# A DLRM tower with a third-order interaction network: another order in the first DMA queues, copies and picks, and picked lines with the row within the line innermost

## The chip, the cores and the metric

The kernel runs on one core of a Trainium2 chip. The metric is the device time of one execution in microseconds (us).

## What is computed

For each of 1024 samples, 32 embedding rows of 16 numbers are gathered from 32 tables. Three layers of a compressed interaction network follow, each a contraction of the outer product of the first rows with the last layer's rows, then a multi-layer perceptron:

```python
e = stack([tbl_m[ids[:, m]] for m in range(32)], axis=1)      # 1024 x 32 x 16
x0 = xk = e
for W in (W0, W1, W2):                                        # (32, 32 or 64, 64)
    xk = relu(einsum('bmd,bhd,mhk->bkd', x0, xk, W))
    outs.append(sum(xk, axis=2))
h = concatenate([*outs, dense_ctx], axis=1)                   # 1024 x 208
h = relu(h @ W_top1 + b_top1); h = relu(h @ W_top2 + b_top2); y = h @ W_top3
```

All of it is in float32. The tables have 1000, 1250, 12500 or 125000 rows.

## The kernel before

**Tiles and phases.** The batch is cut into eight tiles of 128 samples (i), each into two sides (A, Bs) of 64 samples, which are 1024 columns (sample, d). One side of one layer is a phase, written (i, layer, side). `PHASES` sets their order by hand: (0,0,A), (0,1,A), (0,0,Bs), (0,2,A), (0,1,Bs), (1,0,A), (0,2,Bs) and so on. In a phase the rows of xk lie in two PSUM banks, which ScalarE fills (`fill_first`, `fill_second`). VectorE multiplies them by slots of `x0rep`, the rows of x0 spread over the partitions (L1110), into a ring of six z buffers; GpSimd does some of the products of layers 1 and 2 (L554). TensorE multiplies each z by a tile of weights and accumulates (L753); in layer 0 the squares are added before the last step (L749). ScalarE copies the result out (`evacuate`, L861 and L867). VectorE waits to reuse a z buffer until TensorE has finished the step six before.

**Gathers and picks.** Each of the tables with 125000 or 12500 rows is read by indirect DMAs from GpSimd (L504). A small table can be picked instead: it is loaded whole as 125 lines of 8 or 10 rows (`load_lines`, L385). `split_ids` divides the indices into a line and a rest, `spread_lines` (L648) and `find_lines` (L1004) make a one-hot matrix of the lines, and `pick` (L662) multiplies it by the loaded lines. `clear_others` (L1031) multiplies the result by a mask of the row within the line, and `take_rows` (L1044) sums over the 8 or 10 rows. There are ten such groups, q = 0 to 9: six of tile 0, which need all six groups of lines, and four of tile 1. `pick_rows(q)` on VectorE is clear_others(q), find_rows(q+1), find_lines(q+2), take_rows(q).

**The round trip of tile 0.** SyncE saves the even rows of tile 0 to `x0_rows` in HBM once the gathers of those rows have landed and picks 0 to 2 are taken (`save_first(0)`, L457), waits until they have landed, and loads the even slots of side A (`load_x0`, L428). Then it loads six pieces of w0, and does the same for the odd rows, which need picks 0 to 5. The two first bank fills of phase (0,0,A) do not wait for this trip: TensorE turns the rows (`turn_rows`, L677), ScalarE copies them (`copy_rows`, L784) and TensorE selects them (`select_rows`, L689). Phase (0,0,A) uses slots 0, 2, 1 and 1, so its third product needs the first odd slot. After the odd slots come rows, lay and the eight slots of side Bs (`load_side`), the weights of the perceptron (L470 to L475), and tile 1's save (L405).

**Weights.** w0 is summed from w0a and w0b on VectorE, written twice to HBM (`w0_twice`, L400), and loaded in 16 pieces with rotations (`load_w0`, L379), ten by ScalarE's queue and six by SyncE's. w1 and w2 are each loaded in 12 pieces, eight straight from the input (`STRAIGHT`) and four from a copy in HBM with shifted tiles, `w1_wrap` and `w2_wrap` (`make_wrap`, L765; `load_w`, L776). ScalarE's queue issues them all: w1's between the two copy_rows and after the second; w2's behind the bank fills of phase (0,1,A), where ScalarE then waits for the copy to land. Behind w2's loads stands ctx (L937), and behind that ScalarE's work for phase (0,0,Bs). TensorE waits for w1_in before phase (0,1,A), for w2_in before (0,2,A).

**Order on TensorE at the start.**

```python
spread_lines(6)
pick(3)
turn_rows(0)
pick(4)
spread_lines(7)
select_rows(0)
pick(5)
```

## Time and profile before

| | us |
|---|---|
| median of 3 runs | 629.13 |
| lowest and highest | 628.42, 631.07 |
| the profiled execution | 629.63 |
| its span | 627.7 |
| TensorE, VectorE busy | 585.6 (93%), 577.4 (92%) |
| GpSimd, ScalarE busy | 497.3 (79%), 349.6 (56%) |
| mean granted clock of TensorE | 0.984 |

The span is what the profile covers; 1.9 us of the execution's time lie around it. Of the 95.36 MB that the DMA engines move, 90.55 MB are in the queue of SyncE and 2.41 MB in that of ScalarE. A timeline row shows a run of like instructions with the start of the first; the idle time in brackets is that of the engine before it, with what ended it, and "issue" there means that the profile shows nothing that the engine waited for, often its own DMA issues.

### The profile page before, as it was taken

Reading aid. Unit: us, or ns where it says so; the run is one execution under the profiler, and the core shown is the slowest. Engines: PE = TensorE matmul, PEld = TensorE weight load, DVE = VectorE, ACT = ScalarE, POOL = GpSimd, SP = SyncE. Lnnn points to the kernel's source line nnn. Section 1 sums busy time; section 2 is a strip of 40 time slices with the busy share of each in tenths; the row PEclk is TensorE's granted clock in tenths of the full one; section 3 lists DMA queues with packets and bytes.
Section 4 is the critical chain, followed back from the end, with each engine's and each line's share of the span. In section 5 each row is a group of like instructions: output and inputs, shape, how many; then the busy total and the mean of one; then the engine's idle time right before and its main releaser. Section 6 shows DMA issues by size and latency. Waiting matters only on the chain. (4 is left out here: it accounts for less than half of the span.)

```text
span 627.7 us, 8728 instructions
## 1 busy us (share of the span) xinstructions
PE 585.6 (93%) x3126; PEld 214.1 (34%) x3126; DVE 577.4 (92%) x582; ACT 349.6 (56%) x535; POOL 497.3 (79%) x349
## 2 busy tenths in 40 slices
PE   3485689999999899999999999999999999999998
PEld 3361223222442224322342224322442234333444
DVE  5567599899999999999999999999999999999993
ACT  0105174745755667635755666635755666756741
POOL 6753579799888988899888988898888896668770
PEclk9879979999999999999999999999999999999999
DMA  4689979940499928993599727980699728990000
GB/s 110 129 165 236 251 119 272 294 118 4 77 237 224 191 19 185 231 240 58 81 243 247 159 28 198 296 210 3 114 236 242 138 28 202 237 247 3 1 2 1
DMA packets 89326, 95.36 MB, mean 152 GB/s; under 512 B 59597, under 2 KB 68338, under 8 KB 89282
## 3 DMA queue, kind: packets, MB, share of 16 engines
q1 hardware_dynamic: 78590, 90.55, 62.8%
q0 software_dynamic: 7104, 1.83, 3.9%
q10 hardware_dynamic: 3588, 2.41, 1.5%
q8 instruction: 25, 0.41, 0.3%
q14 instruction: 19, 0.16, 0.1%
HBM read 91.35 MB, written 3.94 MB: 152 GB/s over the span
## 5 line engine op out<-in xcount | busy, mean ns | idle before, releaser
L1110 DVE TENSOR_TENSOR z<-xk,x0rep 128x1024 f32<-128x1024 f32 x457 | 522.9, 1223 | 19.8 <-issue 9.6
L753 PE MATMUL acc<-z,w_sb 128*64 128x512 f32 x1828 | 433.6, 599 | 20.4 <-DVE z L1110 17.3
L554 POOL TENSOR_TENSOR z_pool<-x0rep,xk_copy 128x1024 f32<-128x1024 f32 x119 | 283.3, 2381 | 55.7 <-PE acc L753 27.9
L504 POOL DMA_INDIRECT emb<-tbl,idx x222 | 213.0, 959 | 58.4 <-issue 48.3
L753 PEld LDWEIGHTS acc<-z,w_sb 128*64 128x64 f32 x1828 | 123.7, 137 | 294.9 <-issue 161.2
L847 ACT ACTIVATE xk<-xk_copy 32x1024 f32<-32x1024 f32 x128 | 130.5, 1019 | 94.3 <-DVE z L1110 93.1
L753 PE MATMUL acc<-z_pool,w_sb 128*64 128x512 f32 x476 | 122.5, 593 | 0.0
L861 ACT ACTIVATE xk_copy<-acc 64x512 f32<-64x512 f32 x128 | 75.2, 588 | 3.7 <-PE acc L753 2.2
L842 ACT ACTIVATE xk<-lay 128x1024 f32<-128x1024 f32 x15 | 15.4, 1027 | 75.7 <-DVE z L1110 75.7
L753 PEld LDWEIGHTS acc<-z_pool,w_sb 128*64 128x64 f32 x476 | 33.7, 137 | 65.1 <-issue 62.8
L823 ACT ACTIVATE xk<-xk_copy 128x1024 f32<-128x1024 f32 x31 | 31.9, 1028 | 14.2 <-DVE z L1110 13.9
L1083 DVE TENSOR_REDUCE row_sums<-layer_out 128x32 f32<-128x512 f32 x47 | 32.2, 684 | 0.0
L805 ACT ACTIVATE squares<-squares 32x1024 f32<-32x1024 f32 x16 | 16.8, 1050 | 23.4 <-issue 14.5
L867 ACT ACTIVATE layer_out<-acc 128x512 f32<-128x512 f32 x47 | 27.8, 591 | 2.1 <-PE acc L753 1.4
L879 ACT ACTIVATE in<-row_sums 64x32 f32<-64x32 f32 x94 | 21.3, 227 | 4.7 <-DVE row_sums L1083 3.6
L1031 DVE TENSOR_TENSOR x0rep<-acc,mask 128x480 f32<-128x480 f32 (+1 forms) x10 | 6.7, 666 | 14.2 <-PE acc L662 14.2
L662 PE MATMUL acc<-x0rep 125*128 125x160 f32 (+1 forms) x68 | 14.8, 377 | 4.9 <-DMA x0rep<-tbl 4.9
L749 PE MATMUL acc<-squares,w0d_sb 128*64 128x512 f32 x64 | 16.9, 606 | 0.4
L823 ACT ACTIVATE xk<-lay 128x1024 f32<-128x1024 f32 x15 | 15.4, 1028 | 2.8 <-DMA lay<-x_rows 2.4
L784 ACT ACT_TABLE_LOAD x1 | 1.3, 1283 | 27.5 <-issue 27.5
L662 PEld LDWEIGHTS acc<-x0rep 125*128 125x128 f32 x68 | 12.6, 259 | 7.9 <-DMA x0rep<-tbl 5.3
L590 PEld LDWEIGHTS top<-h,wt_sb 128*64 128x64 f32 x224 | 12.7, 137 | 4.0 <-issue 4.0
(67 smaller groups left out, 140.6 us busy)
## 6 DMA issues: line engine op xcount, KB each, us to landing
x0rep<-x_rows SPq DMA_DIRECT2D x128, 512.0 KB, 20.7
lay<-x_rows SPq DMA_DIRECT2D x30, 512.0 KB, 6.9
emb<-tbl,idx POOLq DMA_INDIRECT x222, 3.5
squares<-x_rows SPq DMA_DIRECT2D x16, 128.0 KB, 8.6
x_rows<-emb SPq DMA_DIRECT2D x7, 256.0 KB, 4.6
x_rows<-emb SPq DMA_DIRECT2D x9, 128.0 KB, 5.9
w_wrap<-w ACTq DMA_DIRECT2D x4, 128.0 KB, 9.7
w_sb<-w ACTq DMA_DIRECT2D x8, 64.0 KB
```

Source lines behind the costliest of these rows:

```text
L504: pool.indirect_dma_start(out=emb[:, i % 2, m, :], out_offset=None, in_=tables[m], in_offset=bass.IndirectOffsetOnAxis(ap=idx[:, i, m:m + ...
L554: pool.tensor_mul(z_pool[:, (count - 1) % POOL_RING, :], x0rep[:, g % X0_GROUPS, slot, :], xk_copy[:, side, :]).then_inc(z_pool_ready, 1)
L662: op = pe.matmul(acc[:, ACC_AT[q], t * n * D:(t + 1) * n * D], hots[:, q % HOTS, t * P:(t + 1) * P], lines[:, ALL_PICKED.index(m), 0:n * D ...
L749: pe.matmul(bank[c * H:(c + 1) * H, :], w0d_sb[:], squares[:, side, c * COLS:(c + 1) * COLS], start=False, stop=False)
L753: mm = pe.matmul(bank[c * H:(c + 1) * H, :], w[:, tile, :], src[:, c * COLS:(c + 1) * COLS], start=(k == 0), stop=last)
L823: act.activation(xk[:, 0, :], src, ACT.Copy).then_inc(xk_ready[0], 1)
L847: op = act.activation(xk[q * Q:(q + 1) * Q, 1, :], xk_copy[other * Q:(other + 1) * Q, side, :], ACT.Copy)
L861: op = act.activation(xk_copy[half * H:(half + 1) * H, side, c * COLS:(c + 1) * COLS], bank[c * H:(c + 1) * H, :], ACT.Relu)
L867: act.activation(layer_out[:, n % OUTS, :], bank, ACT.Relu).then_inc(acc_taken, 1)
L879: op = act.activation(dst[:, at:at + ROWS], row_sums[c * H:(c + 1) * H, i % 2, row, :], ACT.Copy)
L1083: dve.tensor_reduce(row_sums[:, i % 2, SUM_ROWS.index((layer, side)), :], layer_out[:, n % OUTS, :].rearrange("p (b d) -> p b d", d=D), AX ...
L1110: dve.tensor_mul(z[:, (count - 1) % RING, :], xk[:, bank, :], src).then_inc(z_ready, 1)
```

## The change

It has four parts. In the pick, the loaded lines are read with the row within the line innermost, so that the product in PSUM, its masked copy and the sum in `take_rows` have the rows to be summed next to each other. On SyncE the lines of group 0 come before w0a and w0b, only tile 1's indices come early (a semaphore of their own, `idx_second_in`), the two writes of w0_twice come after the lines of group 1, and behind the last lines come w1_wrap's copies and the rest of the indices. SyncE issues w0's pieces 12 to 15, of which two stand before its wait for the even rows, and makes w2_wrap ahead of side Bs. On ScalarE w0's pieces 8 to 11 and half of w1's straight pieces come before the second copy_rows, the other half after it, and w1's wrapped pieces after the first square. TensorE does picks 3, 4 and 5 earlier, and VectorE splits tile 1's indices after pick 2.

```diff
@@ -200,7 +200,7 @@
 FIRST_GATHERS = [[m for m in GATHERED[0] if m % 2 == odd] for odd in range(2)]
 FIRST_SAVES = 4
 
-W0_LOADS = 10
+W0_LOADS = 12
 
 LOADED_BY_ACT = (0, 2, 18, 22, 4, 8, 7, 13, 23, 25)
 N_TOP_LOADS = 6
@@ -378,6 +379,12 @@
                 tiles = w0_sb[r::PER_GROUP, 0:TILES0:TILES0 - 1, :] if shift % 2 == 0 else w0_sb[r::PER_GROUP, 1:3, :]
                 queue.dma_start(tiles, rows.rearrange("(g e) k -> g e k", e=2)).then_inc(w0_in, 16)
 
+        def make_wrap(queue, wrap, src, done):
+
+            for at, t in ((0, TILES - WRAP // 2), (WRAP // 2, 0)):
+                queue.dma_start(bass.AP(wrap, at * H, [[WRAP * H, P], [1, WRAP // 2 * H]]),
+                                src[:, t:t + WRAP // 2, :].rearrange("p t k -> p (t k)")).then_inc(done, 16)
+
         def load_lines(queue, by_act, g):
 
             for m in of_group(g)[0]:
@@ -389,15 +396,18 @@
         def _(sp):
 
             sp.dma_start(idx[:, 0, :], ids[0:P, :]).then_inc(idx_first_in, 16)
+            load_lines(sp, False, 0)
             for dst, src in ((w0a_sb, w0a), (w0b_sb, w0b)):
                 sp.dma_start(dst, src).then_inc(w0ab_in, 16)
-            load_lines(sp, False, 0)
-            sp.dma_start(idx[:, 1:NT, :], ids[P:B, :].rearrange("(t p) m -> p t m", p=P)).then_inc(idx_in, 16)
-            for g in range(1, len(PICKED)):
-                load_lines(sp, False, g)
+            sp.dma_start(idx[:, 1, :], ids[P:2 * P, :]).then_inc(idx_second_in, 16)
+            load_lines(sp, False, 1)
             sp.wait_ge(w0_summed, 2)
             for n in range(2):
                 sp.dma_start(w0_twice[:, n, :].rearrange("q (r t k) -> q r t k", r=M, t=TILES0), w0a_sb).then_inc(w0_twice_in, 16)
+            for g in range(2, len(PICKED)):
+                load_lines(sp, False, g)
+            make_wrap(sp, w1_wrap, w1, w1_wrap_in)
+            sp.dma_start(idx[:, 2:NT, :], ids[2 * P:B, :].rearrange("(t p) m -> p t m", p=P)).then_inc(idx_in, 16)
 
             def save_x0(i, lo, hi, row, done):
 
@@ -455,17 +465,21 @@
                 for lo, hi, row in ((0, M, odd), (0, X_ROWS - M, M + odd)):
                     dst = bass.AP(x0_rows, row * PITCH, [[D, P], [2 * PITCH, (hi - lo) // 2], [1, D]])
                     sp.dma_start(dst, emb[:, 0, lo + odd:hi:2, :]).then_inc(saved_first, 16)
-                sp.wait_ge(saved_first, 32 * (odd + 1))
 
             save_first(0)
+            sp.wait_ge(w0_twice_in, 32)
+            load_w0(sp, W0_LOADS, W0_LOADS + 2)
+            sp.wait_ge(saved_first, 32)
             for slot in range(0, SLOTS, 2):
                 load_x0(0, A, slot)
-            load_w0(sp, W0_LOADS, TILES0 * P // M)
+            load_w0(sp, W0_LOADS + 2, TILES0 * P // M)
             save_first(1)
+            sp.wait_ge(saved_first, 64)
             for slot in range(1, SLOTS, 2):
                 load_x0(0, A, slot)
                 if slot == 1:
                     load_rows(0, A)
+            make_wrap(sp, w2_wrap, w2, w2_wrap_in)
             load_side(0, Bs)
             sp.dma_start(wt1_sb[:, 0, :], wt1[0:P, :]).then_inc(top_in, 16)
             sp.dma_start(wt1_sb[0:K3, 1, :], wt1[P:P + K3, :]).then_inc(top_in, 16)
@@ -519,7 +533,7 @@
             for g, group in enumerate(FIRST_GATHERS):
                 for m in group:
                     gather(0, m, gathered_first[g])
-            pool.wait_ge(idx_in, 16)
+            pool.wait_ge(idx_second_in, 16)
             for m in GATHERED[1]:
                 gather(1, m, gathered[1])
 
@@ -528,6 +542,7 @@
                 if m == 0:
 
                     if j == 2:
+                        pool.wait_ge(idx_in, 16)
                         pool.wait_ge(saved_first, 16 * FIRST_SAVES)
                     else:
                         pool.wait_ge(x0_saved[j % 2], 32 * ((j - 1) // 2))
@@ -660,7 +675,8 @@
                     pe.wait_ge(cleared_out, earlier_user(ACC_AT, q))
                 for t, m in enumerate(group):
                     op = pe.matmul(acc[:, ACC_AT[q], t * n * D:(t + 1) * n * D], hots[:, q % HOTS, t * P:(t + 1) * P],
-                                   lines[:, ALL_PICKED.index(m), 0:n * D], start=True, stop=True)
+                                   lines[:, ALL_PICKED.index(m), 0:n * D].rearrange("p (j d) -> p d j", d=D),
+                                   start=True, stop=True)
                 op.then_inc(picked, 1)
 
             def turn_rows(odd):
@@ -698,15 +714,15 @@
             pick(1)
             spread_lines(5)
             pick(2)
+            pick(3)
+            pick(4)
             spread_lines(6)
-            pick(3)
             turn_rows(0)
-            pick(4)
+            pick(5)
             spread_lines(7)
             select_rows(0)
-            pick(5)
+            pick(6)
             spread_lines(8)
-            pick(6)
             turn_rows(1)
             pick(7)
             spread_lines(9)
@@ -759,12 +775,6 @@
 
         @block.scalar
         def _(act):
-            def make_wrap(wrap, src, done):
-
-                for at, t in ((0, TILES - WRAP // 2), (WRAP // 2, 0)):
-                    act.dma_start(bass.AP(wrap, at * H, [[WRAP * H, P], [1, WRAP // 2 * H]]),
-                                  src[:, t:t + WRAP // 2, :].rearrange("p t k -> p (t k)")).then_inc(done, 16)
-
             def load_w(dst, src, tiles, done, pieces):
 
                 half = SLOTS // 2
@@ -789,14 +799,12 @@
             act.wait_ge(cleared, 1)
             act.dma_start(w0d_sb[0:M, :], w0d).then_inc(w0d_in, 16)
             act.wait_ge(w0_twice_in, 32)
-            load_w0(act, 0, W0_LOADS - 2)
+            load_w0(act, 0, 8)
             copy_rows(0)
-            load_w0(act, W0_LOADS - 2, W0_LOADS)
-            make_wrap(w1_wrap, w1, w1_wrap_in)
-            load_w(w1_sb, w1.tensor, TILES, w1_in, STRAIGHT)
+            load_w0(act, 8, W0_LOADS)
+            load_w(w1_sb, w1.tensor, TILES, w1_in, STRAIGHT[:2])
             copy_rows(1)
-            act.wait_ge(w1_wrap_in, 32)
-            load_w(w1_sb, w1_wrap, WRAP, w1_in, WRAPPED)
+            load_w(w1_sb, w1.tensor, TILES, w1_in, STRAIGHT[2:])
 
             def square(i, side):
 
@@ -805,6 +813,8 @@
                 act.activation(of_side, of_side, ACT.Square).then_inc(squares_ready, 1)
 
             square(0, A)
+            act.wait_ge(w1_wrap_in, 32)
+            load_w(w1_sb, w1_wrap, WRAP, w1_in, WRAPPED)
 
             def fill_first(n):
                 if PHASES[n] in TURNED:
@@ -928,7 +938,6 @@
                     take_h2(before_top)
                 fill_second(n)
                 if n == 1:
-                    make_wrap(w2_wrap, w2, w2_wrap_in)
 
                     act.wait_ge(x0_in[0][SLOTS - 1], 16)
                     load_w(w2_sb, w2.tensor, TILES, w2_in, STRAIGHT)
@@ -1028,17 +1037,18 @@
                 dve.wait_ge(picked, q + 1)
                 dve.wait_ge(masked, q + 1)
                 wide = count * n * D
-                dve.tensor_tensor(chosen[:, q % 2, 0:wide].rearrange("p (r d) -> p r d", d=D),
-                                  acc[:, ACC_AT[q], 0:wide].rearrange("p (r d) -> p r d", d=D),
-                                  mask[:, q % 2, 0:count * n].unsqueeze(2).to_broadcast([P, count * n, D]), ALU.mult
-                                  ).then_inc(cleared_out, 1)
+                shape = [P, count, D, n]
+                dve.tensor_tensor(chosen[:, q % 2, 0:wide].rearrange("p (t d j) -> p t d j", d=D, j=n),
+                                  acc[:, ACC_AT[q], 0:wide].rearrange("p (t d j) -> p t d j", d=D, j=n),
+                                  mask[:, q % 2, 0:count * n].rearrange("p (t j) -> p t j", j=n).unsqueeze(2).to_broadcast(shape),
+                                  ALU.mult).then_inc(cleared_out, 1)
 
             def take_rows(q):
 
                 i, g = PICKS[q]
                 _, count, n, _ = of_group(g)
                 dve.wait_ge(cleared_out, q + 1)
-                rows = chosen[:, q % 2, 0:count * n * D].rearrange("p (t j d) -> p t d j", j=n, d=D)
+                rows = chosen[:, q % 2, 0:count * n * D].rearrange("p (t d j) -> p t d j", j=n, d=D)
                 at = 0
                 for run in PICKED[g]:
                     op = dve.tensor_reduce(run_of(emb[:, i], run), rows[:, at:at + len(run)], AX_X, ALU.add)
@@ -1066,9 +1076,10 @@
             last = P - M
             dve.tensor_add(w0a_sb[0:last, TILES0 - 1, :], w0a_sb[0:last, TILES0 - 1, :],
                            w0b_sb[0:last, TILES0 - 1, :]).then_inc(w0_summed, 1)
-            dve.wait_ge(idx_in, 16)
-            split_ids(1)
             for q in range(7):
+                if q == 3:
+                    dve.wait_ge(idx_second_in, 16)
+                    split_ids(1)
                 pick_rows(q)
 
             dve.wait_ge(w0_twice_in, 32)
```

How the order moves on TensorE around pick 5 (L662 and L677 are the picks, L648 and L663 the spread, L689 and L705 select_rows). Before:

```order
L662 MATMUL acc<-x0rep 128x160 x3
L677 MATMUL xk<-ident_f,emb 16x64 x16
L662 MATMUL acc<-x0rep 128x160 x3
L648 MATMUL top<-ident_b,line 125x128 x4
L689 MATMUL xk<-lay,select 64x512 x4
L662 MATMUL acc<-x0rep 128x160 x3
L648 MATMUL top<-ident_b,line 125x128 x3
```

And in the changed kernel:

```order
L677 MATMUL acc<-x0rep 128x160 x9
L663 MATMUL top<-ident_b,line 125x128 x4
L693 MATMUL xk<-ident_f,emb 16x64 x16
L677 MATMUL acc<-x0rep 128x160 x3
L663 MATMUL top<-ident_b,line 125x128 x4
L705 MATMUL xk<-lay,select 64x512 x4
L677 MATMUL acc<-x0rep 128x128 x4
```

Pick 5 stood behind the first select_rows and now stands right behind turn_rows.

SyncE's queue from the last tables (x0rep<-tbl, 125x160) to the save of the odd rows (the second pair of x_rows<-emb). Before:

```order
L385 DMA x0rep<-tbl 125x160 x6
L400 DMA w_twice<-z 4x32x256 x2
L457 DMA x_rows<-emb 128x16x16
L457 DMA x_rows<-emb 128x8x16
L428 DMA x0rep<-x_rows 128x1x1024 x4
L379 DMA w_sb<-w_twice 16x2x64 x6
L457 DMA x_rows<-emb 128x16x16
L457 DMA x_rows<-emb 128x8x16
```

And in the changed kernel:

```order
L406 DMA w_twice<-z 4x32x256 x2
L392 DMA x0rep<-tbl 125x160 x6
L385 DMA w_wrap<-w 128x256 x2
L410 DMA idx<-ids 128x6x32
L467 DMA x_rows<-emb 128x16x16
L467 DMA x_rows<-emb 128x8x16
L380 DMA w_sb<-w_twice 16x2x64 x2
L438 DMA x0rep<-x_rows 128x1x1024 x4
L380 DMA w_sb<-w_twice 16x2x64 x2
L467 DMA x_rows<-emb 128x16x16
L467 DMA x_rows<-emb 128x8x16
```

The two copies into w_wrap and most of the indices are now ahead of the even save, and four instead of six w0 pieces ahead of the odd one.

ScalarE from the last of w1's loads, behind the second copy_rows, to the load of ctx; w1 stands before the fill L831 or L841 and w2 behind it. Before:

```order
L776 DMA w_sb<-w_wrap 32x1x256 x4
L805 ACTIVATE squares<-squares 32x1024
L831 ACTIVATE xk<-acc 64x512 x2
L861 ACTIVATE xk_copy<-acc 64x512 x4
L867 ACTIVATE layer_out<-acc 128x512
L847 ACTIVATE xk<-xk_copy 32x1024 x4
L765 DMA w_wrap<-w 128x256 x2
L776 DMA w_sb<-w 64x1x256 x2
L776 DMA w_sb<-w 32x1x256 x4
L776 DMA w_sb<-w 64x1x256 x2
L776 DMA w_sb<-w_wrap 32x1x256 x4
L937 DMA in<-ctx_t 16x128
```

And in the changed kernel:

```order
L786 DMA w_sb<-w 64x1x256 x2
L813 ACTIVATE squares<-squares 32x1024
L786 DMA w_sb<-w_wrap 32x1x256 x4
L841 ACTIVATE xk<-acc 64x512 x2
L871 ACTIVATE xk_copy<-acc 64x512 x4
L877 ACTIVATE layer_out<-acc 128x512
L857 ACTIVATE xk<-xk_copy 32x1024 x4
L786 DMA w_sb<-w 64x1x256 x2
L786 DMA w_sb<-w 32x1x256 x4
L786 DMA w_sb<-w 64x1x256 x2
L786 DMA w_sb<-w_wrap 32x1x256 x4
L946 DMA in<-ctx_t 16x128
```

The copies into w_wrap are gone from this queue, and w1's loads from w_wrap stand behind the square.

## Rows read from the trace of the kernel before

**Rows 1.** Windows: stretch, length, busy us of PE, PEld, DVE, ACT, POOL, clock, DMA share, GB/s.

```profile
26.00:38.00 12.00, 6.51 (x20) 3.29 (x21) 2.41 (x6) 2.29 (x2) 9.02 (x10) 0.53 1.00 222
...
62.00:78.00 16.00, 10.52 (x48) 3.35 (x48) 9.26 (x9) 2.02 (x3) 9.36 (x7) 1.00 1.05 252
...
78.00:90.00 12.00, 9.78 (x34) 3.05 (x36) 11.65 (x11) 11.79 (x18) 7.90 (x6) 0.72 0.89 143
...
110.00:627.00 517.00, 508.62 (x2736) 177.70 (x2732) 497.66 (x464) 315.52 (x494) 426.08 (x284) 1.00 0.66 145
```

**Rows 2.** Timeline, VectorE: start, us, line, operation, count [idle before <- releaser].

```profile
10.59 0.40 DVE L985 TENSOR_SCALAR quotient<-idx 128x32 f32<-128x32 int32 x2 [3.40 <-DMA idx<-ids]
...
35.42 0.66 DVE L1031 TENSOR_TENSOR x0rep<-acc,mask 128x480 f32<-128x480 f32 x1 [9.87 <-PE acc L662]
...
48.37 2.36 DVE L1110 TENSOR_TENSOR z<-xk,x0rep 128x1024 f32<-128x1024 f32 x2 [0.36 <-DMA x0rep<-x_rows]
...
78.15 4.62 DVE L1110 TENSOR_TENSOR z<-xk,x0rep 128x1024 f32<-128x1024 f32 x4 [6.88 <-issue]
...
82.97 9.14 DVE L1110 TENSOR_TENSOR z<-xk,x0rep 128x1024 f32<-128x1024 f32 x8 [0.20 <-ACT xk L823]
...
119.15 3.49 DVE L1110 TENSOR_TENSOR z<-xk,x0rep 128x1024 f32<-128x1024 f32 x3 [2.63 <-ACT xk L823]
```

**Rows 3.** Timeline, SyncE's queue: start, us that the issues took, line, count.

```profile
24.42 3.66 SPq L428 DMA_DIRECT2D x0rep<-x_rows  x4
...
37.91 2.63 SPq L457 DMA_DIRECT2D x_rows<-emb  x2
...
42.94 0.55 SPq L428 DMA_DIRECT2D x0rep<-x_rows  x1
```

**Rows 4.** DMA issues at 24.6 to 25.8 and at 37 to 39: KB each, us to landing.

```profile
x0rep<-x_rows SPq DMA_DIRECT2D x3, 512.0 KB, 9.8
...
x_rows<-emb SPq DMA_DIRECT2D x1, 128.0 KB, 4.3
```

**Rows 5.** Timeline, TensorE's matmuls.

```profile
51.69 1.03 PE L753 MATMUL acc<-z,w_sb 128*64 128x512 f32 x4
...
55.59 4.38 PE L753 MATMUL acc<-z,w_sb 128*64 128x512 f32 x16 [2.88 <-DVE z L1110]
...
62.81 1.08 PE L753 MATMUL acc<-z,w_sb 128*64 128x512 f32 x4 [2.84 <-DVE z L1110]
...
79.52 5.39 PE L753 MATMUL acc<-z,w_sb 128*64 128x512 f32 x12 [6.19 <-DVE z L1110]
...
87.36 2.79 PE L753 MATMUL acc<-z,w_sb 128*64 128x512 f32 x12 [0.70 <-DMA w_sb<-w_wrap]
```

**Rows 6.** Timeline, ScalarE and its queue.

```profile
41.88 2.60 ACTq L776 DMA_DIRECT2D w_sb<-w_wrap  x4
...
49.55 1.05 ACT L805 ACTIVATE squares<-squares 32x1024 f32<-32x1024 f32 x1 [6.66 <-DMA squares<-x_rows]
...
56.88 0.56 ACTq L765 DMA_DIRECT2D w_wrap<-w  x1
...
70.68 5.23 ACTq L937 DMA_DIRECT2D in<-ctx_t  x1
...
75.95 1.05 ACT L805 ACTIVATE squares<-squares 32x1024 f32<-32x1024 f32 x1 [14.52 <-issue]
```

**Rows 7.** The tile w_wrap: time from issue to landing of its four copies.

```profile
DMA to landing us min/median/max: 8.9/9.7/10.6
```

**Rows 8.** Groups: busy us, mean ns | idle before; the last by shape, 0 to 52 us.

```profile
L842 ACT ACTIVATE xk<-lay 128x1024 f32<-128x1024 f32 x15 | 15.4, 1027 | 75.7 <-DVE z L1110 75.7
...
L1083 DVE TENSOR_REDUCE row_sums<-layer_out 128x32 f32<-128x512 f32 x47 | 32.2, 684 | 0.0
...
L662 PE MATMUL acc<-x0rep 125*128 125x160 f32 (+1 forms) x68 | 14.8, 377 | 4.9 <-DMA x0rep<-tbl 4.9
...
L1044 DVE TENSOR_REDUCE emb<-x0rep 128x64 f32<-128x512 f32 x2 | 2.0, 1000 | 0.0
```

More of the change, by code:

```diff
@@ L298, in build @@
         idx_first_in = sem("idx_first_in")
+        idx_second_in = sem("idx_second_in")
         idx_in = sem("idx_in")
```

## The prediction, made before the changed kernel ran

> **What bounds the kernel now.** I read the windows first. From 110 us to the end TensorE is busy for 508.62 of 517.00 us and VectorE for 497.66, at a full clock and with the DMA engines at 0.66 [rows 1]. Nothing in the diff touches an instruction of that stretch, so the change can only move the moment at which it begins; what it brings is the shift of the whole steady part. Before it things look different: from 26 to 38 us VectorE works 2.41 of 12 us while the DMA engines are at 1.00 and TensorE's clock at 0.53, and from 62 to 78 us the DMA share is 1.05 with TensorE busy 10.52 of 16 [rows 1]. So the second view is VectorE's timeline, for the waits that end late. It waits 3.40 us for the indices, 9.87 us for a pick at 35.42, then for the first odd slot of x0rep (the product at 48.37), 6.88 us before 78.15, and 2.63 us before 119.15 [rows 2]. A wait counts only if nothing else would have held the next step. For that I read SyncE's queue: even slots issued from 24.42, save of the odd rows at 37.91, first odd slot at 42.94 [rows 3]. That last chain leads straight to 48.37. The 6.88 us have another origin: ScalarE fills the banks for phase (0,0,Bs) only after its queue has issued everything for w2, and there it waits 14.52 us of issue, until 75.91 [rows 6].
>
> **The change part by part.** The sum is made against the profiled execution, 629.63 us; the median of the runs shown is 629.13, 0.5 below.
>
> *Indices and lines.* idx for tile 1 comes alone and split_ids(1) moves behind pick 2. The 3.40 us go from VectorE, but the even save is still held by the queue: the order of SyncE now has two w1_wrap copies and the rest of the indices ahead of it, some three more issues of about 0.65 us, as four of 2.60 us show [rows 6], and their bytes. In the old order the lines and w0_twice stood there. I take 24.42 for the even landing unchanged: term 0, bounds -3 (the wait gone in full) and +2 (three issues and the copies' bytes in front).
>
> *Sums over neighbours.* A take of 512 elements costs 1000 ns with the lines' rows outermost [rows 8]; a reduction of as many contiguous elements costs 684 ns [rows 8]. Over ten picks, at up to 1.0 us each, this frees about 3 us of VectorE, all of it before the product at 48.37, which waits for a DMA. What hides it is the x0_rows round trip; term 0, and if that cover went, -3. The other side of the same edit: the 68 pick matmuls, busy 14.8 us together [rows 8], now read their moving operand with a stride of 64 bytes. The trace has no such matmul. Bounds: nothing, or twice the time, which for the 40 of the first six picks is 40 x 14.8/68 = 8.7 us more. I take nothing, since between picks TensorE waits anyway (9.87 us on VectorE's side come from elsewhere); the high end would put picked_out 6 near 33, still ahead of the odd save's turn below. The Trainium skill (SBUF — State Buffer, "Door 1: The DMA port swizzle") says that consecutive SBUF accesses run at full rate only inside a 16-byte line, so that fp32 is free up to a stride of four. The pair 1000 and 684 ns agrees with it, and by that rule the matmuls pay, and the sum stays as it is because they are covered.
>
> *Pick 5 ahead of select_rows(0).* Pick 5 was stuck behind select_rows(0), which waited for ScalarE's copy. It now runs right behind turn_rows(0), and VectorE ends pick 5 near 24 to 26 instead of after its product of 35.42 [rows 2]. SyncE gets to the odd save after four slot loads (3.66 us from 24.42) and two of the former six w0 loads, at about 29 instead of 37.91 [rows 3]: 8 to 9 us earlier. That is one bound. The other is the DMA: the even slots issued at about 25 land 9.8 us later [rows 4], in a stretch at share 1.00 [rows 1], and the odd save stands behind them in the same queue. With w1's straight loads now beside them I expect the slots done at 36 to 37, and with 4.3 us for the save [rows 4] the odd rows land near 41 instead of 42.94. Bounds -8.5 and 0; I take -2, because the share of 1.00 is the nearer row.
>
> *TensorE's clock.* With the picks over by about 37, TensorE idles until the first odd slot. At 78.15 the trace shows what a gap does: 6.19 us idle, and then 12 matmuls in 5.39 us, where 12 at 87.36 take 2.79 [rows 5]; the granted clock is 0.72 from 78 to 90 [rows 1]. The tail of phase 0 is 12 such matmuls, which end at 52.72 [rows 5]. If the clock is at its lower level there, +2.6 at most, and if not, 0. I take +2. So phase 0 ends about where it does now.
>
> *w1_wrap's loads behind square(0, A).* Four issues, 2.60 us [rows 6], move behind a square that waits for the odd rows. Behind them on ScalarE stands the first fill of phase 1. The square ran from 49.55 to 50.60 [rows 6] and the fill can start at 52.72, so the delay is about half a microsecond: term 0. When they land is the first rival.
>
> *w2_wrap's copies on SyncE.* ScalarE no longer issues them at 56.88 nor waits for them; that wait ended near 68, since four more loads, 2.60 us, came before ctx at 70.68 [rows 6]. Its twelve loads at 0.65 us each are now done near 65. Then comes the load of ctx, which took 5.23 us to issue [rows 6], because the queue was full; I keep that, so ScalarE is free near 71 instead of 75.91: 5 us. The product at 82.97 came 7.06 us behind 75.91; it would come near 78.2. The limit of this term is TensorE, whose last matmul of phase 1 ends at 79.52 - 6.19 = 73.33 [rows 5]. Three activations of about 1.03 us [rows 8] no longer stand between it and the copy-out, so 73.33 + 7.06 - 3.1 = 77.3 is the earliest: bounds -5.7 and 0, taken -4.7.
>
> *w2_in.* TensorE waits for it until 87.36 [rows 5]. The last of twelve loads was issued just before ctx at 70.68 [rows 6], 16.7 us earlier. The two copies that stood ahead of them landed 9.7 us after their issue [rows 7]; without them the twelve gain between 0 and 9.7 us, and I take the middle, 4.5, since their bytes still pass the same engines from SyncE's queue. From there to 119.15 TensorE has no gap, so its -4.5 and VectorE's -4.7 are one gain, not two.
>
> *Last wait of the indices, POOL, tile 1.* GpSimd's gathers of tile 2 also wait for idx_in, issued before 20 us and used after 40: 0. Tile 1's rows come from the same queue, and between 82.97 and 119.15 VectorE's only longer wait is one for ScalarE [rows 2]: 0.
>
> Sum: 0 + 0 - 2 + 2 + 0 - 4.5 = -4.5, that is 625.1 against the profiled run and **624.6** against the median.
>
> **The rivals.** *A, w1 late (slower).* Place: TensorE's wait for w1_in before phase 1. Its first four products took from 55.59 to 59.97, and then it idled 2.84 us until 62.81 [rows 5]; so it bears a start up to 59.3. The wrapped loads were issued at 41.88; now at about 50 to 53. With 9.7 us to landing [rows 7] w1_in comes at 62, with the 16.7 us of w2's at 69. In the latter case phase 1 ends 10 us later, w2's gain is covered by it, the idle gap adds some 2.6 us of low clock, and the product of 82.97 comes near 90: 629.1 + 7 = 636. At 62 about 2.7 us (62 less 59.3) and a low clock are lost and the total is 627 to 629. For it: the queue of SyncE is full when they go out, as at 62 to 78 with a share of 1.05 [rows 1]. Against it: the loads are small, and at 41.88 they had landed before 55.59.
> *B, the round trip is freed.* SyncE's order decides and not the bytes: -8.5 at the odd save, no cold clock, then -4.5: 616.
> *C, ScalarE's queue gets its share.* The Trainium skill (DMA: Bandwidth & Descriptors, "Queues, rings and completion order") says that each engine takes turns between queues packet by packet. As a mechanism here: the twelve loads no longer wait behind SyncE's, so w2_in comes 9 us earlier, and then 77.3 and the 2.63 us before 119.15 [rows 2] are what is left to gain: 5.7 + 2.6 = 8.3, 621. Rows 7 speak against it with 9.7 us for two copies of 128 KB.
> *D, nothing.* ctx's issue ends when the DMA backlog ends, at 75.9 whatever stands before it, and the change moves no bytes away: 629.
>
> **How the numbers follow.** A difference of 0.5%, 3.1 us, is about what a measurement of this kernel can tell from none. Forecast 0.40, A 0.14 (its worse half slower, its better half the same), B 0.13, C 0.13, D 0.20. Faster by over 0.5%, below 626.0: B, C and most of the forecast, with an edge of D, 0.60. Slower, above 632.3: 0.12. The rest, 0.28, is within 0.5%. The range goes from B's edge, 617, to 631: A's worse half and the outer part of B are left out. The forecast alone stands at 621.5 to 627.5.
>
> **What would show it.** VectorE's 9.87 us before pick 5 gone; takes of 512 elements near 0.68 us; the odd save issued near 29 but landed near 41; a product at about 46.5 with a long DMA wait before it; a lower clock around 50; ScalarE free at about 71; the products of (0,2,A) from about 78; w2_in near 83. It is wrong if the odd save lands before 38 (B), if TensorE's first matmul of phase 1 comes after 60 (A), if w2_in comes before 80 (C), or if ctx's issue still ends at 75 to 76 (D).

## The result and the profile after

The changed kernel takes 633.14 us in the median of 9 runs (629.83 to 635.59), the kernel before 629.66 us of 9 (628.42 to 632.04). The ratio is 1.0045, with a 95% interval of 1.0024 to 1.0066: about 0.45% slower, inside the 0.5% called "same" in the prediction, and above the end of its range (631.0). The forecast of 624.6 was wrong in sign.

The profiled execution of the changed kernel is the lowest of its nine runs, 629.83 us with a span of 628.0; that of before took 629.63. The spans alone would say that nothing happened. So the start is compared by its milestones; why the spans agree is told in the last part.

VectorE's timeline of the changed kernel (start, us, line, operation, count, in brackets the idle time before it and what ended it), which answers to [rows 2]:

```profile
14.22 0.67 DVE L1054 TENSOR_REDUCE emb<-x0rep 128x64 f32<-128x512 f32 x1
...
25.98 0.66 DVE L1041 TENSOR_TENSOR x0rep<-acc,mask 128x480 f32<-128x480 f32 x1 [0.67 <-PE acc L677]
...
47.02 2.36 DVE L1121 TENSOR_TENSOR z<-xk,x0rep 128x1024 f32<-128x1024 f32 x2 [6.80 <-DMA x0rep<-x_rows]
...
53.21 1.42 DVE L1105 TENSOR_SCALAR xk<-acc 64x512 f32<-64x512 f32 x2 [2.58 <-PE acc L769]
...
76.00 4.62 DVE L1121 TENSOR_TENSOR z<-xk,x0rep 128x1024 f32<-128x1024 f32 x4 [0.15 <-issue]
...
85.67 9.14 DVE L1121 TENSOR_TENSOR z<-xk,x0rep 128x1024 f32<-128x1024 f32 x8 [5.06 <-ACT xk L833]
...
121.15 1.23 DVE L1121 TENSOR_TENSOR z<-xk,x0rep 128x1024 f32<-128x1024 f32 x1 [1.93 <-ACT xk L833]
```

The take of 512 elements is down to 0.67 us; the 9.87 us before pick 5 are down to 0.67 (the row of 25.98), and a wait of 6.80 us for the first odd slot stands in their place. The product at 47.02 is 1.35 us earlier than before. The product for (0,0,Bs) is earlier too, at 76.00 instead of 78.15. But the one for (0,2,A), behind a wait for ScalarE's fill, starts at 85.67 instead of 82.97, and the one near 120 at 121.15 instead of 119.15. These last 2.0 us are what the start lost.

SyncE's queue of the same kernel, against [rows 3]:

```profile
25.17 3.29 SPq L438 DMA_DIRECT2D x0rep<-x_rows  x4
...
29.88 7.95 SPq L467 DMA_DIRECT2D x_rows<-emb  x2
41.56 0.55 SPq L438 DMA_DIRECT2D x0rep<-x_rows  x1
```

The save of the odd rows is issued from 29.88 instead of 37.91, and the first odd slot follows at 41.56 instead of 42.94: the queue gave 8 us and the DMA engines kept 6.6 of them.

TensorE's matmuls, against [rows 5]:

```profile
48.30 1.97 PE L769 MATMUL acc<-z,w_sb 128*64 128x512 f32 x4 [5.10 <-DVE z L1121]
50.06 1.92 PE L765 MATMUL acc<-squares,w0d_sb 128*64 128x512 f32 x4
...
65.78 6.37 PE L769 MATMUL acc<-z,w_sb 128*64 128x512 f32 x20 [12.62 <-DMA w_sb<-w_wrap]
...
88.62 2.79 PE L769 MATMUL acc<-z,w_sb 128*64 128x512 f32 x12 [2.73 <-DMA w_sb<-w_wrap]
```

Phase 1 began at 55.59; now it waits 12.62 us for w1's wrapped pieces, until 65.78. The second wait is for w2, and it ends at 88.62 instead of 87.36. ScalarE and its queue, against [rows 6]:

```profile
47.86 2.60 ACTq L786 DMA_DIRECT2D w_sb<-w_wrap  x4
...
62.84 8.19 ACTq L786 DMA_DIRECT2D w_sb<-w_wrap  x4
71.07 2.68 ACTq L946 DMA_DIRECT2D in<-ctx_t  x1
73.80 1.05 ACT L813 ACTIVATE squares<-squares 32x1024 f32<-32x1024 f32 x1 [11.91 <-issue]
```

and of before, the row that [rows 6] does not have:

```profile
68.05 2.60 ACTq L776 DMA_DIRECT2D w_sb<-w_wrap  x4
```

w1's four loads of 32 KB leave at 47.86 to 50.5 and are there at 65.78, over 15 us later. w2's four wrapped loads now begin at 62.84 instead of 68.05, but their issue takes 8.19 us instead of 2.60, so that the last is out at 71.03, where before it was out at 70.65. ScalarE stands free 2.15 us earlier (73.80 instead of 75.95), for ctx takes 2.68 instead of 5.23 us. The windows (stretch, length, busy us of PE, PEld, DVE, ACT, POOL, clock, DMA share, GB/s), against [rows 1]:

```profile
26.00:38.00 12.00, 12.00 (x78) 8.52 (x76) 8.15 (x18) 1.01 (x1) 9.20 (x10) 0.86 1.05 211
...
50.00:62.00 12.00, 3.16 (x10) 0.70 (x6) 6.68 (x8) 8.17 (x11) 4.55 (x3) 0.64 1.05 239
```

From 26 to 38 us VectorE works 8.15 us instead of 2.41, and from 50 to 62 us TensorE is busy for 3.16 us of 12, at a granted clock of 0.64, with a DMA share of 1.05.

### The profile page after: what moved, and what is told of

Same layout as the page of the kernel before. It is cut to its first block, busy times and chain, and to the rows that moved or that the text cites. A ratio compares the mean times of both kernels' runs of the same rounds, so it can differ in the third digit from the quotient of the medians.

```text
span 628.0 us, 8730 instructions
## 1 busy us (share of the span) xinstructions
PE 589.0 (94%) x3126; PEld 218.8 (35%) x3126; DVE 574.4 (91%) x582; ACT 349.9 (56%) x535; POOL 497.1 (79%) x349
## 4 chain that ended last, share of the span: by engine, by line
PE 44%; DVE 10%; issue 2%; ACT 1%; DVEq 0%
PE acc L769 39%; DVE z L1121 9%; PE top L605 1%; PE acc L765 1%; DVE row_sums L1094 1%; PE top L596 1%; PE top L593 1%; ACT xk L833 1%; PE acc L645 0%; ACT xk L852 0%; PE top L614 0%; PE xk L633 0%; PE xk L625 0%; PE top L580 0%; PE top L650 0%
## 5 line engine op out<-in xcount | busy, mean ns | idle before, releaser
L1121 DVE TENSOR_TENSOR z<-xk,x0rep 128x1024 f32<-128x1024 f32 x457 | 524.5, 1260 | 25.8 <-ACT xk L833 7.0
L769 PE MATMUL acc<-z,w_sb 128*64 128x512 f32 x1828 | 433.9, 600 | 25.8 <-DMA w_sb<-w_wrap 15.4
L769 PEld LDWEIGHTS acc<-z,w_sb 128*64 128x64 f32 x1828 | 125.1, 137 | 299.9 <-issue 168.5
L1094 DVE TENSOR_REDUCE row_sums<-layer_out 128x32 f32<-128x512 f32 x47 | 33.9, 721 | 0.0
L677 PE MATMUL acc<-x0rep 125*128 125x160 f32 (+1 forms) x68 | 18.8, 436 | 5.8 <-DMA x0rep<-tbl 5.8
L677 PEld LDWEIGHTS acc<-x0rep 125*128 125x128 f32 x68 | 15.1, 263 | 9.0 <-DMA x0rep<-tbl 6.3
L605 PE MATMUL top<-h,wt_sb 128*64 128x128 f32 x224 | 13.4, 273 | 0.0
```

What stands on the lines that cost most here:

```text
L605: last = pe.matmul(top[halves[half], m * P:(m + 1) * P], wt2_sb[:, k, columns_of(m, half)], h1[:, k, :], start=(k == 0), stop=(k == F1 // ...
L677: op = pe.matmul(acc[:, ACC_AT[q], t * n * D:(t + 1) * n * D], hots[:, q % HOTS, t * P:(t + 1) * P], lines[:, ALL_PICKED.index(m), 0:n * D ...
L769: mm = pe.matmul(bank[c * H:(c + 1) * H, :], w[:, tile, :], src[:, c * COLS:(c + 1) * COLS], start=(k == 0), stop=last)
L1094: dve.tensor_reduce(row_sums[:, i % 2, SUM_ROWS.index((layer, side)), :], layer_out[:, n % OUTS, :].rearrange("p (b d) -> p b d", d=D), AX ...
L1121: dve.tensor_mul(z[:, (count - 1) % RING, :], xk[:, bank, :], src).then_inc(z_ready, 1)
```

## The experiments

Open were the cost of w1's late loads, why w2 did not come earlier, and which of the two sets the end. "w1 ahead" puts w1's wrapped loads back ahead of the square; "w2 on SyncE" takes w2's loads out of ScalarE's queue. Each ratio is against the kernel before on the same chip. The chips are numbered in the order of these runs; the first comparison is not counted among them.

### First chip: parts alone

w1 ahead, in the changed kernel:

```diff
             load_w(w1_sb, w1.tensor, TILES, w1_in, STRAIGHT[2:])
+            act.wait_ge(w1_wrap_in, 32)
+            load_w(w1_sb, w1_wrap, WRAP, w1_in, WRAPPED)
...
             square(0, A)
-            act.wait_ge(w1_wrap_in, 32)
-            load_w(w1_sb, w1_wrap, WRAP, w1_in, WRAPPED)
```

> The changed kernel with one thing put back: w1's four wrapped loads stand ahead of the first square again. Theory 'w1 late' (the 12.62 us for which TensorE waits before phase (0,1,A) are what the change gives back): that wait is gone, phase 1's first matmul comes at about 54.7 as the z of the changed kernel allow (54.67), its last near 74. Then w2_in is the next bound: its loads were last seen to land at 88.6, so phase (0,2,A) starts on TensorE at 84 to 88, and the kernel is 2 to 6 us faster than the changed one, 627 to 631. Rival 'another cause' (the wait is covered, or the picks' new layout or the queue order costs it): it stays within 1 us of the changed kernel, 632 to 634.

Measured: 650.33 us against 653.54, 0.9951 (0.9924 to 0.9977). Here the edit did not take the wait away: its loads go out only from 62.14, and TensorE still waits 13.40 us for them, until 85.28. So this run says nothing of what that wait costs.

With w2's two copies on ScalarE's queue again (`make_wrap(sp, w2_wrap, ...)` back to `make_wrap(act, ...)` behind the fills):

> e1_w1_ahead, and w2_wrap's two copies back on ScalarE's queue, as in the kernel before. Theory 'the copies on SyncE free ScalarE' (my term of -4.7 us): ScalarE's square for (0,0,Bs) goes back from about 72 to 75 or later, the products of (0,0,Bs) start 3 to 5 us later than in e1_w1_ahead. If w2_in decides the end of it, the total is only 0 to 2 us above e1_w1_ahead; if ScalarE decides, 4 us above. Rival 'w2's data are what counts': with the copies back on ScalarE's queue w2_in lands later by the bytes' time, 1 to 5 us, and so does the total.

Measured: 1.0018 (0.9993 to 1.0043), 0.7% above the one without it. On this chip the copies on SyncE did help.

The kernel before, with w1's wrapped loads behind the square (the first diff the other way round):

> The kernel before with only w1's four wrapped loads moved behind the first square. Theory 'w1 late': issued at about 50.6 they land at 60 to 68; TensorE bears a start of phase 1 up to 59.3, so phase 1 ends 1 to 9 us later; with the low clock the kernel is 3 to 9 us slower than before, 632 to 638. Rival 'it needs the rest of the change' (w2's copies on SyncE ahead of side Bs push them back): they land before 60 and the time stays at 629 to 630.

Measured: 1.0056 (1.003 to 1.0083).

The changed kernel with the old layout of the pick in the matmul, the masking and the take:

```diff
-                                   lines[:, ALL_PICKED.index(m), 0:n * D].rearrange("p (j d) -> p d j", d=D),
+                                   lines[:, ALL_PICKED.index(m), 0:n * D],
...
-                rows = chosen[:, q % 2, 0:count * n * D].rearrange("p (t d j) -> p t d j", j=n, d=D)
+                rows = chosen[:, q % 2, 0:count * n * D].rearrange("p (t j d) -> p t d j", j=n, d=D)
```

> The changed kernel with the old layout of the picks (row within the line outermost, sums over strided elements). Theory 'covered': takes of 512 elements go back from 0.67 to 1.0 us, VectorE is up to 3 us later through the picks, and the product behind the first odd slot still starts at 47, since the save waits for the DMA queue: the time stays within 1 us of the changed kernel, 632 to 634. Rival 'the sums count': 2 to 3 us slower. Rival 'strided reading costs TensorE': 1 to 3 us faster.

Measured: 0.9945 (0.9916 to 0.9974). What this is to be held against came with the next chip.

All times of this chip are some 24 us above those of the first comparison, those of the kernel before too (653.54 against 629.66). VectorE's timeline of the kernel with w1 ahead shows where:

```profile
35.05 0.66 DVE L1041 TENSOR_TENSOR x0rep<-acc,mask 128x480 f32<-128x480 f32 x1 [18.80 <-remote]
```

Between two picks VectorE stands still for 15 to 20 us in the runs of this chip. The profile names no engine and no transfer of this core as what ended the wait, only "remote"; TensorE's 15.72 us in the same stretch have only "issue". The kernel before with w1 late shows it too (16.13 us on VectorE before 36.16).

### Second chip: the same stall again

The changed kernel, the one with w1 ahead, w1 ahead with the perceptron's six loads behind tile 1's side A, and w1 ahead with 22 matmuls into an unused bank that fill TensorE's gap before the third step of phase 0:

> The changed kernel itself, beside the ones that follow, since the chip of the first four runs was 24 us slower for every kernel and had waits in the picks that the first traces do not have. Theory 'w1 late': on a chip like the first, TensorE waits about 12 us before phase (0,1,A) and the ratio to before is about 1.004; on one like the second the picks end near 50, everything of the start comes in one heap, w1 waits longer still, and the ratio is anything from 0.99 to 1.01.

> w1's wrapped loads ahead of the first square, again. On a chip like the first they are issued at about 36 instead of 47.9, before SyncE's loads of side Bs, and land before 50: TensorE's 12.62 us are gone, phase 1 starts at 54 to 55, and w2_in (88.6 in the changed kernel) is what is left: 2 to 6 us faster than the changed kernel, ratio to before 0.995 to 1.001. On a chip like the second it changes little against the changed kernel, since the picks hold copy_rows(1) back until 59 and the loads go out at 62 in either order.

> f1_w1_ahead, and the perceptron's weights (1 MB in six loads on SyncE's queue) moved from behind side Bs to behind tile 1's side A. Theory 'the DMA queue of SyncE holds w2': less stands in the queue between 54 and 85 us, w2_in lands 2 to 5 us earlier and tile 1's save starts near 68 instead of 79.7; 1 to 4 us faster than f1_w1_ahead. Rival: w2 waits for side Bs alone, and the time stays.

> f1_w1_ahead with 22 extra matmuls of 256 columns on w0 into the unused bank top, before the third step of phase (0,0,A), to keep TensorE from idling there (their result is not used). Theory 'the clock falls in the gap': the 5.10 us gap before 48.30 is filled, the twelve matmuls of the tail of phase 0 take about 3.1 us instead of 4.9, and phase 1 starts 1 to 2 us earlier; the total is 0 to 2 us below f1_w1_ahead. Rival: the tail is covered by w1_in or w2_in, and the total does not move.

| kernel | us | ratio to before (656.18) | interval |
|---|---|---|---|
| changed | 652.65 | 0.9944 | 0.9917 to 0.9972 |
| w1 ahead | 654.02 | 0.9965 | 0.9937 to 0.9992 |
| w1 ahead, perceptron's weights late | 649.99 | 0.9915 | 0.9882 to 0.9947 |
| w1 ahead, gap filled | 654.0 | 0.9973 | 0.9941 to 1.0005 |

The stall is here again, 22.10 us on VectorE before 43.56 with w1 ahead. On this chip the changed kernel is faster than before, and w1 ahead adds nothing, though here it does take the wait for w1 away (12.59 us before 90.49 in the changed kernel, none in this one): a wait of 5.60 us for w2 follows. The old layout at 0.9945 on the first such chip equals the new at 0.9944 on this one, so no effect of the layout is seen, though the two were not run on the same chip. Filling the gap brought nothing either. It did what it was meant to, the twelve matmuls of the tail took 2.74 us from 74.78 instead of 5.38 from 73.39 with w1 ahead, but TensorE then waited 5.99 us for w1: the low clock behind the gap is not what the time hangs on. Only 0.93 MB out of the way of w2 brought something, 0.5% below w1 ahead, with intervals that just overlap.

### Third chip: without the stall

Changed, w1 ahead, the kernel before with w1 late, and w1 ahead with the perceptron's weights late and ctx moved from ScalarE's queue to SyncE's behind them:

> The changed kernel beside g1 to g3. Where the picks run without the stall (the save of the odd rows issued near 30), TensorE waits 12 to 13 us for w1's wrapped loads and the ratio to before is 1.002 to 1.007. Where they stall, 0.992 to 0.997 as before.

> w1's wrapped loads ahead of the first square. Without the stall: loads issued near 36, phase 1 starts at 54 to 56, 2 to 6 us faster than g0_changed. With the stall: within 2 us of g0_changed.

> The kernel before with w1's wrapped loads behind the first square alone. Theory 'w1 late': 3 to 9 us slower than before in either case (1.0056 on the first chip with the stall). Rival: the wait is covered where nothing stalls, and the time is that of before.

> f2_top_late with the first ctx load on SyncE's queue as well, behind the perceptron's weights. ScalarE then has nothing behind w2's loads before the square of (0,0,Bs), which took 2.7 to 5.2 us to issue. Theory: the fills of (0,0,Bs) come 2 to 3 us earlier, but TensorE's end of phase 1 and w2_in stand next, so 0 to 2 us on f2's 0.9915: 0.988 to 0.992 with the stall, 0.985 to 0.995 without it. Rival: w2_in alone decides and ctx brings nothing.

| kernel | us | ratio to before (629.89) | interval |
|---|---|---|---|
| changed | 631.92 | 1.0038 | 1.0012 to 1.0064 |
| w1 ahead | 632.58 | 1.0056 | 1.0034 to 1.0078 |
| before, w1 late | 635.41 | 1.0105 | 1.0079 to 1.013 |
| w1 ahead, weights late, ctx on SyncE | 629.87 | 0.9994 | 0.9969 to 1.002 |

The result comes back (1.0038 beside 1.0045). In the kernel before, w1 late costs 1.05%; TensorE there waits 15.94 us before 69.71. In the changed kernel, taking it away brings nothing, where 2 to 6 us were expected; the last kernel misses its range (0.985 to 0.995) as well. TensorE's timeline with w1 ahead says why:

```profile
57.49 5.53 PE L769 MATMUL acc<-z,w_sb 128*64 128x512 f32 x16 [2.88 <-DVE z L1121]
...
87.72 5.33 PE L769 MATMUL acc<-z,w_sb 128*64 128x512 f32 x12 [5.52 <-DMA w_sb<-w_wrap]
```

The 12.6 us before phase 1 are gone, it begins at 57.49, and all of it comes back in waits, the last of them for w2, which ends at 87.72 as ever (87.36 before, 88.25 in the changed kernel on this chip). The longer wait of 5.52 us also costs clock: 12 matmuls take 5.33 us, where behind a wait of 2.73 us they took 2.79. So the product near 120 comes at 122.04, later than the changed kernel's 120.78 on this chip. ScalarE's queue of this kernel:

```profile
64.28 6.43 ACTq L786 DMA_DIRECT2D w_sb<-w_wrap  x4
```

Again the last of w2's loads is out at 70.71. In three kernels with starts at 62.84, 64.28 and 68.05 it is 71.03, 70.71 and 70.65: the end of the issue does not follow its start, and 17 us later the data are there. The two DMA queues from 58.8 to 87.7 us show what goes on meanwhile (queue, kind, packets, MB, share of the 16 engines' time; q1 is SyncE's, q10 ScalarE's):

```profile
q1 hardware_dynamic: 5863, 5.63, 93.7%
q10 hardware_dynamic: 608, 0.53, 7.7%
```

w2's twelve loads and ctx are 0.53 MB together. They are neither held back as a whole nor let past: beside SyncE's full queue they get 7.7% of the engines' time, in packets of some 0.9 KB, and take the whole 29 us. What sets this share no run shows. In the fourth kernel the perceptron's weights are not in SyncE's queue there, w2 is there at 84.46, and the ratio is 0.6% below that of w1 ahead.

### Fourth chip: w2 between the slots of side Bs

If w2's landing is the bound, its loads have to go in the queue of the bulk, ahead of most of it, and not beside it. `load_side` for tile 0's side Bs issues them, and ScalarE's queue none of them:

```diff
                     load_x0(i, side, slot)
                     if slot == 1 and i == 0:
                         load_lay(i, side, 1)
+                    if i == 0 and slot == 2:
+                        load_w(sp, w2_sb, w2.tensor, TILES, w2_in, STRAIGHT)
+                    if i == 0 and slot == 4:
+                        sp.wait_ge(w2_wrap_in, 32)
+                        load_w(sp, w2_sb, w2_wrap, WRAP, w2_in, WRAPPED)
+                        sp.dma_start(in3[H:K3, :], ctx_t[:, 0:P]).then_inc(ctx_in, 16)
```

> The changed kernel with w1's wrapped loads ahead of the square, and w2's twelve loads and ctx issued by SyncE between the slots of side Bs (straight behind slot 2, wrapped behind slot 4). Theory 'w2 landing is the bound, and it is late because 4 MB of side Bs stand ahead of it in the DMA engines': w2_in before 80 us instead of 87.7, TensorE's wait of 5.5 us before (0,2,A) below 1 us, the square of side Bs near 68 to 70, the total 3 to 6 us below the kernel with w1 ahead, ratio to before 0.996 to 1.000. Rival 'the bytes bound the start, whatever their order': TensorE waits as long, now for the late slots of side Bs, and the ratio stays 1.003 to 1.007.

> As the one before, with the perceptron's weights behind tile 1's side A as well. Theory 'w2 landing': little beyond the one before, since w2 is ahead of the perceptron's weights now: ratio within 0.002 of it. Rival 'the bytes bound the start': these bytes count wherever they stand, and it is 0.004 to 0.006 below the one before.

> The kernel before with only this: w2's two copies, its twelve loads and ctx issued by SyncE, at the same places. Theory 'w2 landing': w2_in and ScalarE's issue time both go from its path; the product of (0,0,Bs) near 73 to 75 instead of 78.15, (0,2,A) from 80 to 82 instead of 87.36; 4 to 7 us faster, ratio 0.989 to 0.994. Rival 'the bytes bound the start': 0.998 to 1.002.

> The kernel before with w2 on SyncE and the perceptron's weights behind tile 1's side A. Theory 'w2 landing': 0.987 to 0.994, within 0.002 of the one before. Rival 'the bytes bound the start': about 0.004 below the one before.

| kernel | us | ratio to before (630.8) | interval |
|---|---|---|---|
| changed, w1 ahead, w2 on SyncE | 625.75 | 0.9925 | 0.9898 to 0.9952 |
| the same, perceptron's weights late | 626.58 | 0.9937 | 0.9915 to 0.9959 |
| before, w2 on SyncE | 627.57 | 0.9943 | 0.992 to 0.9966 |
| the same, perceptron's weights late | 625.9 | 0.9923 | 0.9893 to 0.9954 |

TensorE, VectorE and SyncE's queue of the first of them:

```profile
80.52 2.96 PE L789 MATMUL acc<-z,w_sb 128*64 128x512 f32 x12 [1.30 <-DMA w_sb<-w_wrap]
```

```profile
78.86 9.14 DVE L1123 TENSOR_TENSOR z<-xk,x0rep 128x1024 f32<-128x1024 f32 x8 [1.64 <-ACT xk L840]
...
114.32 9.14 DVE L1123 TENSOR_TENSOR z<-xk,x0rep 128x1024 f32<-128x1024 f32 x8 [1.92 <-ACT xk L840]
```

```profile
51.35 9.77 SPq L396 DMA_DIRECT2D w_sb<-w  x8
...
62.71 2.62 SPq L396 DMA_DIRECT2D w_sb<-w_wrap  x4
```

The last of w2's loads is out at 65.33 and w2 is there by 80.52, 6.8 us earlier than before; the square of side Bs on ScalarE comes at 62.91. The product near 120 comes at 114.32, 4.8 us before its place in the kernel before, and the medians differ by 5.05 us; 0.9925 is better than the range that was expected (0.996 to 1.000). The start is shorter although the same bytes move, so a start bound by bytes in whatever order is refuted.

The move does two things: w2 lands earlier, and ScalarE has nothing to issue before its square. The last kernel of the third chip parts them. There TensorE ends (0,0,Bs) at 79.18 as here at 79.22, w2 is there at 84.46 instead of 80.52, and the ratio is 0.9994 instead of 0.9925: what is left between them is w2's landing, and the low clock behind the wait for it (12 matmuls in 4.37 instead of 2.96 us). Not tried was w2 early on ScalarE's own queue, so how much the queue does and how much the earlier issue is open. Behind this version the perceptron's weights are worth nothing measurable (the intervals overlap, and the two pairs differ in sign). In the kernel before, the same move alone gives 0.9943, a little above its range (0.989 to 0.994), and (0,2,A) starts there at 82.96. Its difference to the first row is within the intervals, so with w2 and w1 repaired nothing shows that the rest of the change is worth anything.

### Fifth chip: w1 late once more

The last question was whether w1's late loads cost again once w2 does not cover them: the kernel of the fourth chip with w1's wrapped loads behind the square, as the change has them, and that kernel itself.

> The changed kernel with w2's loads and ctx on SyncE between the slots of side Bs, and w1's wrapped loads left behind the square as the change has them. Theory 'two bounds in turn' (w1 late costs only once w2's landing no longer covers it): the wait for w1_in is 8 to 13 us, the start of phase 1 near 63 to 66 instead of 57, no wait for w2_in behind it, and the ratio 0.006 to 0.012 above the next one, so about 0.999 to 1.004. Rival 'w1 late is always covered': the same as the next one within 0.002.

> The same with w1's wrapped loads ahead of the square, a kernel that ran before at 0.9925. Both theories: 0.990 to 0.995 again.

Measured: w1 late 633.22 us, 1.0042 (1.0021 to 1.0063); w1 ahead 627.09 us, 0.9939 (0.9915 to 0.9963), against 630.83. With w1 late TensorE shows

```profile
65.82 7.44 PE L789 MATMUL acc<-z,w_sb 128*64 128x512 f32 x20 [11.42 <-DMA w_sb<-w_wrap]
...
88.15 3.25 PE L789 MATMUL acc<-z,w_sb 128*64 128x512 f32 x12 [1.16 <-DVE z L1123]
```

The wait for w2 is gone, and 1.0% is lost; 1.0042 is at the upper end of what was expected. What w1's four loads wait behind is seen here by itself, since w2 is not in ScalarE's queue. The two queues from 48.4 to 65.8 us:

```profile
q1 hardware_dynamic: 1350, 4.07, 101.2%
q10 hardware_dynamic: 144, 0.13, 3.5%
```

The four loads are the 0.13 MB. From 48.4 to 53 us ScalarE's queue moves no packet, and by the time the last of the 144 has passed, SyncE's queue has moved 4.07 MB. The four corners, ratios of changed kernels to before:

| | w2 on ScalarE's queue | w2 on SyncE's, ahead |
|---|---|---|
| w1 late (as changed) | 1.0038 | 1.0042 |
| w1 ahead | 1.0056 | 0.9925 and 0.9939 |

Either repair alone gives nothing; both together give 1% against the changed kernel, and a kernel that is 0.6 to 0.75% faster than before. The columns are from different chips without the stall, each against the kernel before on its own.

## Why the prediction was wrong

**Right in mechanism and size.** *Pick 5*: -2 taken; the odd slots are issued 1.38 us earlier (41.56), and the product begins 1.35 us earlier. The odd save issued from 29.88 but landed only by 41.56 is what the text described. *Clock*: +2 taken; the last twelve matmuls of phase 0 start at 48.30 and take 4.86 us, four of them 1.92 where four at 51.69 took 1.03 [rows 5]; before, the twelve took 3.07 us from 49.65, so the term is 1.8. VectorE's copy of the result comes at 53.21 instead of 52.76. *Sums over neighbours*: 0; a take costs 0.67 us as forecast, and the wait for the odd slot, 6.80 us, swallows it. The 68 pick matmuls are busy 18.8 us instead of 14.8, far from the high end of twice, with the clock in it; neither side touches the end. *Indices*: even slots at 25.17 instead of 24.42, inside the bounds.

**Half right: w2_wrap's copies, -4.7.** ScalarE is free at 73.80, not at 71. It did come sooner, but the issues of w2's wrapped loads, reckoned at 0.65 us each, took 8.19 us for four in a full queue. I let ctx wait for the backlog and not the loads ahead of it. And the 2.15 us bought nothing, since TensorE ended phase 1 late: ScalarE's copy-out waited for it until 81.63, and VectorE's product for (0,2,A) came at 85.67, not at 78.2.

**Wrong: w2_in, -4.5.** I added the gain of an earlier issue to the landing, from the middle of 0 and 9.7. The lower bound was the truth: the last issue ends at 71.03 (70.65 before), and w2 is there at 88.62 (87.36 before). Rival D named the like, an end set by the backlog whatever stands before it, but I applied it to ctx's issue alone. With this term at 0 the sum has no gain left, whatever w1 does; w1 ahead at 1.0056 shows it.

Rival C, by which ScalarE's queue gets its turn between packets, is refuted as a gain and not as a mechanism. The Trainium skill (DMA: Bandwidth & Descriptors, "Queues, rings and completion order") says that each DMA engine takes turns between queues, a packet at a time. The trace agrees so far as both queues move packets in the same stretch (608 and 5863 from 58.8 to 87.7 us with w1 ahead). But ScalarE's packets carried 0.53 MB to SyncE's 5.63, and such a turn got four loads of 32 KB there over 15 us after their issue.

**Wrong: w1's wrapped loads, 0.** Rival A was the case in mechanism, with a chance of 0.14. It had priced the landing at 9.7 or 16.7 us, and the time from the last issue (50.46) to the start (65.78) is 15.3 us, so near the worse half. Its reckoning also had phase 1 bear a start up to 59.3; the rows it names give 55.59 + 2.84 = 58.4. What held the result at 633 instead of 636 is that in the changed kernel w2 at 88.62 covered most of it: with w2 out of the way the same late loads cost 1.0%. The price was set too low because the row of 41.88 was taken as evidence ("at 41.88 they had landed before 55.59"): in the old order they left ahead of side Bs's eight slots, in the new one beside them. w1 and w2 are a pair of bounds, and the sum had neither: either of them alone was enough to undo the gain, w2 by the 1.0056 of w1 ahead and w1 by the 1.0042 of the fifth chip.

**The sum again** with the measured terms: -1.4 for the odd slots and +1.8 for the low clock, 0.45 us later at phase 0's end, and then w1 late makes the first and w2 the second bound: 88.62 - 87.36 = 1.3 us later for w2, and 2.0 us at the product near 120. The changed kernel's medians lie 3.5 us (first comparison) and 2.0 us (third chip) above before.

## What to carry to other kernels

A small transfer that has to be there early must be issued before the bulk begins, as w1's loads are with w1 ahead: out at 38.25 on ScalarE's queue, landed before SyncE's odd slots and side Bs fill the engines (from 42 to 57 us ScalarE's queue moves 2 packets). If it has to go while the bulk moves, put it into the bulk's own queue at the place where it is needed; the second queue got 7.7% and 3.5% of the engines' time in the two stretches above, and an issue that began earlier only lasted longer. That the bulk's queue as such is what helps was not tried apart from the place in it. When a wait has been repaired and the time does not move, look which wait behind it ends at the same moment as always, and repair both before judging either; a one-at-a-time test here would have discarded 1%. Price a small load moved beside a large block by the time that the block takes to pass, not by the small load's former latency.

## What was not expected

**A short wait decides between executions in the steady part.** The start lost 2.0 us, the two spans differ by 0.3. The sums of layer_out on VectorE show where it went: up to the one at 199.08 (201.06 in the changed kernel) the kernel before leads by 2.0 us, at the next, 219.14 against 219.75, by 0.6, and at 500.40 by 0.45. Between the two stands one row of its timeline:

```profile
207.82 11.41 DVE L1110 TENSOR_TENSOR z<-xk,x0rep 128x1024 f32<-128x1024 f32 x10 [1.11 <-DMA x0rep<-x_rows]
```

The profiled execution of the changed kernel has no such wait; that of w1 late on the fifth chip has two, of 1.20 and 1.44 us, near 210 us. So a single span can carry one to three us of this, and a change in the start is better read from milestones. On each of the last three chips the start of the product near 120 (114.32 to 125.93 us over the ten kernels) stands in the order of the medians.

**Chips with a stall in the picks.** On the first two of the five chips every profiled kernel stood some 15 to 22 us within the picks, with no releaser of its own core, while GpSimd's gathers went on (14.3 of the 19 us from 16 to 35 us on the first). On the second of these chips the change was 0.56% faster (0.9944). Why it does better there and what the stall is stay open; nothing was tried on it.

**What an idle gap costs.** Two waits of TensorE before the same 12 matmuls: 2.73 us and then 2.79 us for them, 5.52 us and then 5.33 us for them. The length of the wait alone does not say it: in the run with w2's copies back on ScalarE's queue 2.15 us were followed by 4.24. The clock granted right behind the longer one, from 88 to 90 us with w1 ahead, is 0.50:

```profile
88.00:90.00 2.00, 2.00 (x6) 0.49 (x6) 0.26 (x1) 0.44 (x1) 1.84 (x2) 0.50 0.53 43
```

That is the level of 1.2 GHz instead of 2.4.
